# Layout turns by the DMA crossbar in a software-pipelined four-network kernel

## The reference

```python
x = x + _L0_xattn_ref(_layernorm(x), ctx, ...)   # 8 heads of 8 channels over t=256, rotary, softmax
x = x + _L0_ffn_ref(_layernorm(x), ...)          # 256 -> 2 x 1024 -> 256, rows rounded to 8 bits, ternary weights
x = x + _L1_xattn_ref(_layernorm(x), ctx, mask)  # one head, 64 x 64 scores, masked softmax
x = x + _L1_ffn_ref(_layernorm(x), ...)          # 256 -> 2 x 1024 -> 256, rms_norm, ternary weights per 64

# the last one
gu = jnp.einsum('bsd,hd->bsh', x, wq_gu)
gate, up = jnp.split(gu, 2, axis=-1)
h = jax.nn.silu(gate) * up
hn = rms_norm(h)
return jnp.einsum('bsh,dh->bsd', hn, wq_p)
```

## Time and profile before

| | |
|---|---|
| median of 3 runs | 987.54 us (986.87 to 994.34) |
| profiled execution | 984.53 us, its span 982.8 us |
| mean granted TensorE clock | 0.927 |
| TensorE, VectorE, ScalarE, GpSimd busy | 84%, 89%, 74%, 67% |
| DMA | 53.2 MB, 54 GB/s |

### The profile page before, as it was taken

The page is one execution under the profiler, slowest core; times in us unless marked ns, Lnnn a source line. Parts: engine busy times, 40 slices in busy tenths (PEclk is TensorE's granted clock), DMA queues, the critical chain, the costliest instruction groups (busy, mean ns, idle before and its releaser), DMA issues. The chain is left out here.

```text
span 982.8 us, 22542 instructions
## 1 busy us (share of the span) xinstructions
PE 828.4 (84%) x7102; PEld 441.8 (45%) x7188; DVE 875.1 (89%) x1846; ACT 723.3 (74%) x1520; POOL 660.5 (67%) x978
## 2 busy tenths in 40 slices
...
DMA packets 78958, 53.21 MB, mean 54 GB/s; under 512 B 20589, under 2 KB 77549, under 8 KB 78841
## 3 DMA queue, kind: packets, MB, share of 16 engines
...
## 5 line engine op out<-in xcount | busy, mean ns | idle before, releaser
L851 DVE TENSOR_REDUCE mx<-psS 128x2 f32<-128x512 f32 x512 | 337.5, 677 | 23.2 <-PE psS L413 21.1
L568 ACT ACTIVATE prob<-psT 128x512 f32<-128x512 f32 x512 | 286.5, 594 | 39.8 <-PE psT L423 35.7
L413 PE MATMUL psS<-KQ 31*128 31x256 f16 x1024 | 170.2, 283 | 52.0 <-DVE mx L851 45.7
L437 PE MATMUL psW<-prob,vst 128*32 128x256 f32 x2048 | 140.2, 392 | 0.0
L423 PE MATMUL psT<-KQ 32*128 32x256 f16 x1024 | 132.1, 277 | 5.0 <-ACT prob L568 5.0
L506 PE MATMUL psW<-guT,xlT 128*128 128x512 bf16 x256 | 98.0, 383 | 4.3 <-DVE xlT L953 2.6
L720 POOL TENSOR_TENSOR hqB<-uB,rnd 128x512 bf16<-128x512 f32 x64 | 65.4, 1043 | 51.9 <-ACT uB L613 51.9
L413 PEld LDWEIGHTS psS<-KQ 31*128 31x128 f16 x1024 | 47.8, 93 | 116.3 <-DVE mx L851 83.1
L506 PE MATMUL psW<-guT,xhT 128*128 128x512 bf16 x227 | 87.4, 385 | 0.0
L742 POOL TENSOR_TENSOR uB<-gB,vB 128x512 f32<-128x512 f32 x64 | 82.6, 1291 | 2.8 <-DVE vB L908 1.9
L437 PEld LDWEIGHTS psW<-prob,vst 128*32 128x32 f32 x2048 | 54.1, 110 | 66.3 <-issue 28.8
(11 more groups left out here) (155 smaller groups left out, 2073.4 us busy)
## 6 DMA issues: line engine op xcount, KB each, us to landing
KQ<-hl SPq DMA_DIRECT2D x192, 64.0 KB, 1.9
...
oR<-rden_d SPq DMA_DIRECT2D x128, 32.0 KB
...
```

What stands on the lines that cost most here:

```text
L413: m = nc.tensor.matmul(psS[:, n % 2, T * k:T * k + T], KQ[p % DEEP][r, 1, g, 128 * k:128 * k + 128], KQ[p % DEEP][r, 0, g, :], start=True, ...
L437: m = nc.tensor.matmul(bank[32 * j:32 * j + 32, :], vst[p % DEEP][:, k, 4 * n + j, :], prob[:, (4 * n + j) % 8, k, :], start=(k == 0), sto ...
L568: m = nc.scalar.activation(flat(prob[:, n % 8, :, :]), psT[:, n % 2, :], ACT.Exp, scale=float(HC) ** -0.5)
L851: m = nc.vector.tensor_reduce(mx[:, p % 2, :, 4 * (n % 4) + n // 4], psS[:, n % 2, :].rearrange("p (c s) -> p c s", c=NK), AX.X, ALU.max)
```

## The change

- The 16-bit matrices xqB (128 x 256), hqB (128 x 1024) and the halves of network C are turned by transposing transfers that SP issues (`dma_start_transpose`), five a pair: qT, ht, xT, hhT, hlT. The TensorE transposes xqT, hqT, x3T and hT and the PSUM copies xqTc and hqTc go.
- Network C splits its rows into halves in SBUF, ahead of the turn: xh (ScalarE) and xl (now GpSimd) from xnC, hh (ScalarE, which applies the row scale as it writes fp16) and hl (VectorE) from hC. hn goes.
- Three multiplies of one or two columns on VectorE (in sxB, sx and rs) become `tensor_scalar` in place of `tensor_tensor`.
- x3 has two buffers. The half tiles lie in free parts of `stage`.
- All five orders and the sharing of the banks are new. Cd, x4 run at shift -8 in place of -7, B one shift earlier, C's layer norm at -6, T and E at -1 and 0.

```diff
     "sp": 
-    """xP:3 st:-8 sg:-2 or:-3 cB:-5 kq:1 ov:-2 xA:-2 md:0 cP:3 d1:-2""",
+    """xP:3 xA:-2 or:-2 xT:-6 md:0 hhT:-7 qT:-3 hlT:-7 ht:-4 cP:3 cB:-4 sg:-1 ov:-1 st:-8 kq:2 d1:-1""",
+    "dve": """mx5:0 mx6:0 wx:-6 vB0:-4 gB0:-4 mx7:0 rs:-6 gB1:-4 mx8:0 aC0:-7 mx9:0 aC1:-7 vB1:-4 x4:-8 mx10:0 x3:-6
+           mx11:0 bsC:-6 x2:-5 mvC:-6 hB0:-4 mx12:0 x1:-3 bsD:-5 bsB:-3 hC0:-7 mvB:-3 rc:-2 hC1:-7 mvD:-5 hB1:-4
+           mx13:0 mx14:0 r1:2 amB:-3 mx15:0 sxB:-3 mx0:1 amH:-4 bsP:3 sx:-4 mx1:1 mx2:1 mvP:3 hl0:-7 hl1:-7 mx3:1
+           mx4:1 msk:-5""",
+    "pe": """T1:-1 Bv0:-4 Bg0:-4 S7:0 S8:0 Bg1:-4 Cg0:-7 Cg1:-7 T2:-1 S9:0 T3:-1 pT:-6 Cd0:-8 Bv1:-4 Cd1:-8 S10:0
+           T4:-1 S11:0 T5:-1 ro:-6 y:-3 Bd:-5 S12:0 T6:-1 T7:-1 S13:0 Cu0:-7 pv0:-1 T8:-1 T9:-1 S14:0 Cu1:-7 pv1:-1
+           proj0:2 T10:-1 T11:-1 proj1:2 S15:0 T12:-1 S0:1 T13:-1 v:2 mxp:0 S1:1 T14:-1 T15:-1 S2:1 pv2:-1 xcT:-5
+           S3:1 S4:1 pv3:-1 sc:-5 S5:1 S6:1 T0:0""",
+    "act": """hi:1 E0:-1 pD:-6 E1:-1 tB0:-4 th0:-7 th1:-7 pTc:-6 E2:-1 E3:-1 E4:-1 E5:-1 E6:-1 E7:-1 tB1:-4 E8:-1
+           sq0:-7 E9:-1 sq1:-7 E10:-1 E11:-1 xh:-6 pc:2 E12:-1 E13:-1 xr:-3 mxc:0 hh0:-7 hh1:-7 xq:-3 E14:-1 E15:-1
+           hr0:-4 hr1:-4 xcTc:-5 u0:-1 vst:2 u1:-1""",
+    "pool": """hq0:-5 hq1:-5 om:-3 lo:1 rsP:2 uB0:-4 xnP:2 uB1:-4 xb:-4 rsC:-6 xnC:-6 rsB:-3 xnB:-3 ms:-7 xl:-6 rsD:-5
+           xnD:-5 r2:2 rot:2""",
...
+                    elif name == "qT":
+                        after_apart(sp, "xq", p)
+                        after_apart(sp, "Bg", p - 1)
+                        after_apart(sp, "Bv", p - 1)
+                        sp.dma_start_transpose(out=xqT[:], in_=xqB[:]).then_inc(S["qT"], 16)
+                    elif name == "ht":
+                        after_apart(sp, "hq", p)
+                        after_apart(sp, "Bd", p - 1)
+                        sp.dma_start_transpose(out=hqT[:], in_=hqB[:]).then_inc(S["ht"], 16)
+                    elif name == "xT":
+                        after_apart(sp, "xh", p)
+                        after_apart(sp, "xl", p)
+                        after_apart(sp, "Cg", p - 1)
+                        after_apart(sp, "Cu", p - 1)
+                        sp.dma_start_transpose(out=xT[:], in_=flat(xhl)).then_inc(S["xT"], 16)
+                    elif name == "hhT":
+                        after_apart(sp, "hh", p)
+                        after_apart(sp, "Cd", p - 1)
+                        sp.dma_start_transpose(out=hhT, in_=flat(hhC)).then_inc(S["hhT"], 16)
+                    elif name == "hlT":
+                        after_apart(sp, "hl", p)
+                        after_apart(sp, "Cd", p - 1)
+                        sp.dma_start_transpose(out=hlT, in_=flat(hlC)).then_inc(S["hlT"], 16)
...
-                        m = nc.scalar.copy(flat(xhT[:]), psW[:, BANK["x3T"], 0:T])
+                        m = nc.scalar.copy(xhl[:, 0, :], xnC[:])
...
-                        m = nc.scalar.activation(hnC[:, n, :], hC[:, n, :], ACT.Copy, scale=msC[:, 2:3])
-                        m = nc.scalar.copy(flat(hhT[:, 4 * n:4 * n + 4, :]), psW[:, BANK[f"hT{n}"], :])
+                        m = nc.scalar.activation(hhC[:, n, :], hC[:, n, :], ACT.Copy, scale=msC[:, 2:3])
...
+                        m = nc.gpsimd.tensor_tensor(xhl[:, 1, :], xnC[:], xhl[:, 0, :], ALU.subtract)
...
-                        nc.vector.tensor_tensor(sB[:, 8:10], gam_q[:, 0:2], sB[:, 1:2].broadcast_to([P, 2]), ALU.mult)
+                        nc.vector.tensor_scalar(sB[:, 8:10], gam_q[:, 0:2], sB[:, 1:2], None, ALU.mult)
...
-                        nc.vector.tensor_tensor(sB[:, 10:11], sB[:, 5:6], gam_q[:, 2:3], ALU.mult)
+                        nc.vector.tensor_scalar(sB[:, 10:11], sB[:, 5:6], gam_q[:, 2:3], None, ALU.mult)
...
-                        m = nc.vector.tensor_tensor(sD[:, 4:5], sD[:, 3:4], valid[:, p:p + 1], ALU.mult)
+                        m = nc.vector.tensor_scalar(sD[:, 4:5], sD[:, 3:4], valid[:, p:p + 1], None, ALU.mult)
...
-                        m = nc.vector.tensor_tensor(hlT[:, 4 * n:4 * n + 4, :].rearrange("p k q -> p (k q)"),
-                                                    psW[:, BANK[f"hT{n}"], :],
-                                                    hhT[:, 4 * n:4 * n + 4, :].rearrange("p k q -> p (k q)"),
-                                                    ALU.subtract)
+                        m = nc.vector.scalar_tensor_tensor(out=hlC[:, n, :], in0=hC[:, n, :], scalar=msC[:, 2:3],
+                                                           in1=hhC[:, n, :], op0=ALU.mult, op1=ALU.subtract)
```

More of the change, by code:

```diff
@@ L64 @@
 ORDER = {
[L65 to L78, removed]
-}
@@ L85 @@
+    "pool": """hq0:-5 hq1:-5 om:-3 lo:1 rsP:2 uB0:-4 xnP:2 uB1:-4 xb:-4 rsC:-6 xnC:-6 rsB:-3 xnB:-3 ms:-7 xl:-6 rsD:-5
+           xnD:-5 r2:2 rot:2""",
+    "sp": """xP:3 xA:-2 or:-2 xT:-6 md:0 hhT:-7 qT:-3 hlT:-7 ht:-4 cP:3 cB:-4 sg:-1 ov:-1 st:-8 kq:2 d1:-1""",
+}
+BANKS = ("Bg0 Cg1 ro pv0",
+         "Bg1 Cd0 Bd Cu1 xcT sc",
+         "Bv0 pT y proj0 v",
+         "Cg0 Bv1 Cu0 proj1 mxp pv2")
 BANK = {name: bank for bank, names in enumerate(BANKS) for name in names.split()}
[L87 to L90, removed]
+READER = {"proj0": "r1", "proj1": "pc", "v": "vst", "mxp": "mxc", "pv0": "u0", "pv2": "u1", "y": "x1",
+          "Bg0": "gB0", "Bg1": "gB1", "Bv0": "vB0", "Bv1": "vB1", "Bd": "x2", "xcT": "xcTc", "sc": "msk",
+          "pT": "pTc", "ro": "x3", "Cg0": "aC0", "Cg1": "aC1", "Cu0": "hC0", "Cu1": "hC1",
+          "Cd0": "x4"}
@@ L454, in body @@
                                                  start=True, stop=True)
[L455 to L459, removed]
                     elif kind in ("Bg", "Bv"):
                         if n == 0:
-                            after(pe, "xqTc", p)
+                            after_dma(pe, "qT", p)
                         if p == 0:
@@ L468, in body @@
                                                  start=(k == 0), stop=(k == NK - 1))
[L469 to L473, removed]
                     elif kind == "Bd":
-                        after(pe, "hqTc", p)
+                        after_dma(pe, "ht", p)
                         for c in range(8):
@@ L494, in body @@
                         m = nc.tensor.matmul(bank[:, 0:T], pTD[:], cB[:], start=True, stop=True)
[L495 to L499, removed]
                     elif kind in ("Cg", "Cu"):
                         if n == 0:
-                            after(pe, "xl", p)
+                            after_dma(pe, "xT", p)
                         w = guT[:, :, HID * (kind == "Cu") + 512 * n:HID * (kind == "Cu") + 512 * n + 512]
                         for k in range(NK):
-                            for part in (xhT, xlT):
-                                m = nc.tensor.matmul(bank, part[:, k, :], w[:, k, :], start=(k == 0 and part is xhT),
-                                                     stop=(k == NK - 1 and part is xlT))
-                    elif kind == "hT":
-                        after(pe, "hn", p, n)
-                        for c in range(4):
-                            m = nc.tensor.transpose(bank[:, 128 * c:128 * c + 128], hnC[:, n, 128 * c:128 * c + 128],
-                                                    ident)
+                            for part in range(2):
+                                m = nc.tensor.matmul(bank, xT[:, NK * part + k, :], w[:, k, :],
+                                                     start=(k == 0 and part == 0), stop=(k == NK - 1 and part == 1))
                     elif kind == "Cd":
-                        after(pe, "hl", p, n)
+                        if n == 0:
+                            after_dma(pe, "hhT", p)
+                            after_dma(pe, "hlT", p)
                         for c in range(4 * n, 4 * n + 4):
```

76 lines of the change are left out of this document (35 added, 41 removed).

## The result

| | before | after |
|---|---|---|
| median of 4 runs each | 987.20 us (986.39 to 994.34) | 1051.69 us (1050.80 to 1052.84) |
| profiled execution, its span | 984.53, 982.8 us | 1050.80, 1049.0 us |
| mean granted TensorE clock | 0.927 | 0.874 |

The ratio is 1.064 (95% interval 1.059 to 1.069): the changed kernel is 64 us slower, where 953 us were forecast, and it lies outside the range.

The account below looks back on a forecast made before the run. VectorE was taken to bound the 24 full passes: 24 x (24.7 - 25.2) = -12 us, fill -4, drain -18, so 984.5 becomes 950.5, plus 3.0 to the median: about 953 us, range 915 to 1040.

Parts of the forecast that it names:

- VectorE without waits: 23.97 us a pass: Full passes: moving xl saves 0.33 us and three column multiplies 0.91, from 25.21 to 23.97 us if nobody waits.
- Bounds: 0 and 4 x 1.06 = 4.2 us. I take 0.7.: VectorE, full passes: four exposed two-input instructions wait for GpSimd's port, 0.7 us a pass, giving a 24.7 us pass.
- The second rival: Full passes: hl0 and hl1 each wait 1.06 us for GpSimd's port, a 26.1 us pass, some 998 us; 12%.
- hl now reads two SBUF tiles, as hB does: nothing: VectorE, twice a pass: hl's new inputs change nothing, median 0.680 us against a mean of 0.680.
- What TensorE or ScalarE lose there is worth nothing by itself.: Full passes, 8 to 31: VectorE alone sets them, so work taken off TensorE or ScalarE gains nothing by itself.
- SP's queue: Full passes: five transposing transfers add 9.5 us, 21.1 in all, below the 24.7 us pass, so they cost nothing.
- The ends of the loop, X = 2.8 and 10.1: Loop rc to vB0: pass at least 17.4 + X (xT's, hhT's issues, qT's landing), so 20.2 or 27.5 us.
- The first rival, the crossbar by the block,: SP's queue: each of 30 blocks costs 0.63 us, the queue's 30.5 us becomes the pass, about 1140 us; 18%.
- Drain: -18: Last passes: the last network's chain is cut, 17 us a pass for 20.5, less an eighth partial pass: -18 us.
- Fill: -4.: First passes, 0 to 7: mostly VectorE's too, eight passes at -0.5 us each, -4 us.

Follow-up runs that it names:

- the dose of the slow hl: Changed kernel with hl only scaling hC, read and written in interleaved order, low half not subtracted: 1102.01 us, ratio 1.117.
- Both orders that I tried: Changed kernel with hl0, hl1 behind aC1 a pass later: 1076.11 us, ratio 1.088; changed kernel with bsP ahead of r1: 1085.41 us, ratio 1.101.

## Why the prediction was wrong

- **VectorE without waits: 23.97 us a pass.** Right to 0.2. The small `tensor_scalar` take 0.21 to 0.23 in place of 0.144 (priced from sx's first instruction, whose scalars are constants and not a column), which makes 24.2. In the shortest pass reached with after's orders, 24.55, VectorE is busy 24.2 us.
- **"Bounds: 0 and 4 x 1.06 = 4.2 us. I take 0.7."** This term failed, by size. The pair hl0, hl1 alone takes 2.0 us too much (3.27 against the 1.25 of the row maxima), of which 0.1 is the form's own (0.745 each without a wait) and 1.9 the wait. The average of before's waits was no measure for two exposed instructions in a row beside two long GpSimd ones. The second rival named this very place and priced it at 2.1 us, and got 12% of the chance. The hl of a row maximum and the dose of the slow hl show the mechanism from both sides.
- **"hl now reads two SBUF tiles, as hB does: nothing".** The row was hB's median, 0.68. But hB has the same form and another neighbour. In after too, hB's median is 0.66 and hl's 1.59. In after hB0 starts just ahead of GpSimd's x1b (509.72 and 509.86), and x1b pays: its median is 1.11 us there and 0.74 before. A form's price holds for its place beside GpSimd, not for its kind.
- **"What TensorE or ScalarE lose there is worth nothing by itself."** The work that left TensorE was worth nothing, and its going cost: with the held VectorE TensorE idled, the clock fell to 0.50 once a pass, and its later products reached VectorE late: 0.8 us. The step missed that cover can run both ways. Of the 3.1 us between VectorE's own 24.2 and 27.32, the pair accounts for 2.0 and the fall for 0.8; 0.3 are not assigned, about what VectorE idles in the passes without a fall too (0.33).
- **SP's queue.** The sum was priced too high (five issues 6.2 us, not 9.5). The ends of the loop, X = 2.8 and 10.1, do not follow from its terms either, which give 2.6 and 9.5; the forecast does not use them. The verdict "costs nothing" held for the full passes, for the wrong reason. The model left out cB's wait for ro, 6.8 us a pass, at the head of the queue. Both orders that I tried ran into this queue, and the 0.9 us that qT's late landing costs without the port lies in it too.
- **The first rival, the crossbar by the block,** is refuted: 8 blocks are issued in 1.25 us, 2 in 1.19. The Trainium skill gives 1309 ns for one block by the crossbar ("VectorE: DVE Perf Modes", section "The three transpose paths"). Here it is not paid by each: 8 blocks land in 3.1 to 3.2 us.
- **Drain: -18.** The last step did get short. Between successive x4 the last eight passes took 24.1, 23.3, 22.8, 23.2, 19.1, 17.6, 15.4 and 14.2 us (before 24.4, 21.9, 22.1, 19.2, 19.8, 19.7, 18.5 and 20.6). Near the end the 14 to 18 of the forecast are there; but four earlier ones stay at 23 to 24, and the eighth, extra pass is added. I had applied the end's loop to all. In the end +3.7.
- **Fill: -4.** It was +14. bsP of pair 1 already starts at 30.5 us in place of 25.5, of pair 3 at 96.8 in place of 88.8, and of pair 5 at 137.6 in place of 125.6. It is so with plain copies too, so it doesn't come from the turning in the transfers; the new orders are what is left, and no run takes them apart. Which step does it was not found, and the cause stays open.
